# Row sums moved to ScalarE's accumulator, and two transposes moved ahead of the output projection, in an attention and FFN layer

## The reference

```
def layer(x):
    n = (x - mean(x)) / sqrt(var(x) + 1e-5)
    q, k, v = n @ Wq + bq, n @ Wk + bk, n @ Wv + bv      # 8 heads of 128
    # attention inside blocks of 64 tokens only
    scores = einsum('bnqhd,bnkhd->bhnqk', q, k) * 128 ** -0.5
    out = einsum('bhnqk,bnkhd->bnqhd', softmax(scores), v)
    x = x + out @ Wo + bo
    n = (x - mean(x)) / sqrt(var(x) + 1e-5)
    y = square(relu(n @ W_fc.T)) @ W_proj.T              # 4096 hidden
    mem, total = 0, 0
    for _ in range(5):
        reset = mem > 1
        mem = 0.9 * mem + y - reset
        total += mem > 1
    return x + total / 5
```

## Time and profile before

| | |
|---|---|
| Median of 2 runs | 1156.52 us (1153.59 to 1159.45) |
| Profiled execution, its own time | 1153.43 us |
| Span of its slowest core (core 2) | 1151.9 us |
| Spans of the 8 cores | 1132.4 to 1151.9 us |
| PE, DVE, ACT, POOL busy | 833.4, 485.1, 393.3, 254.0 us |
| Attention stage on core 2 | from 0 to about 540 us |

### The profile page before, as it was taken

The page is one execution under the profiler, slowest core; times in us unless marked ns, Lnnn a source line. Parts: engine busy times, 40 slices in busy tenths (PEclk is TensorE's granted clock), DMA queues, the critical chain, the costliest instruction groups (busy, mean ns, idle before and its releaser), DMA issues.

```text
span 1151.9 us, 19025 instructions; the slowest of 8 cores (1132.4 to 1151.9 us)
## 1 busy us (share of the span) xinstructions
PE 833.4 (72%) x6624; PEld 603.6 (52%) x6624; DVE 485.1 (42%) x513; ACT 393.3 (34%) x841; POOL 254.0 (22%) x122
## 2 busy tenths in 40 slices
PE   0098459943896379746997979879798897979910
PEld 0044324432343234432786868768687786868800
DVE  0303431153204430434005639275491855739186
ACT  1032323232232313121444444544444444454400
POOL 3000100010000100000003516153260633516154
PEclk9999559955997579859898999999899998999955
DMA  9994770057203640176686949789495996959600
GB/s 155 197 228 78 146 146 1 2 101 144 49 1 72 128 94 0 27 148 192 180 278 198 309 155 316 230 255 326 168 309 188 309 299 200 321 162 324 234 37 37
DMA packets 127291, 194.20 MB, mean 169 GB/s; under 512 B 42208, under 2 KB 44256, under 8 KB 127200
## 3 DMA queue, kind: packets, MB, share of 16 engines
q1 hardware_dynamic: 108144, 151.03, 43.3%
q0 software_dynamic: 14448, 33.56, 16.2%
q10 hardware_dynamic: 4608, 8.39, 2.0%
HBM read 192.95 MB, written 25.17 MB: 189 GB/s over the span
## 4 chain that ended last, share of the span: by engine, by line
PE 60%; DMA 18%; DVE 10%; ACT 5%; issue 4%; SPq 1%; POOL 1%; DVEq 0%; ACTq 0%; POOLq 0%
PE psC L802 17%; DMA w2scratch<-w2stage 10%; PE psA L836 9%; PE psB L836 8%; DMA w1slab<-w1scratch 5%; DMA bv_sb<-bv 3%; PE psA L604 3%; PE psA L336 3%; PE psB L604 2%; PE psB L375 2%; PE psA L356 2%; PE psB L336 2%; PE psA L375 2%; PE psB L356 2%; DVE mem_q L907 2%
## 5 line engine op out<-in xcount | busy, mean ns | idle before, releaser
L802 PE MATMUL psC<-xn2t_sb,w1slab 128*128 128x256 bf16 x2048 | 276.5, 281 | 16.8 <-ACT xn2t_sb L740 10.5
L802 PEld LDWEIGHTS psC<-xn2t_sb,w1slab 128*128 128x128 bf16 x2048 | 205.2, 101 | 48.7 <-issue 19.8
L813 ACT ACTIVATE h_bf<-psC 128x256 bf16<-128x256 f32 x256 | 97.6, 381 | 225.6 <-PE psC L802 225.4
L836 PE MATMUL psA<-h_bf,w2slab 128*128 128x256 bf16 x1024 | 156.1, 276 | 25.2 <-ACT h_bf L816 22.5
L903 POOL TENSOR_TENSOR acc_q<-acc_q,spk_q 128x2048 bf16<-128x2048 bf16 (+1 forms) x27 | 148.4, 5495 | 72.4 <-DVE spk_q L899 72.4
L836 PE MATMUL psB<-h_bf,w2slab 128*128 128x256 bf16 x1024 | 155.7, 275 | 0.0
L907 DVE SCALAR_TENSOR_TENSOR mem_q<-mem_q,y_sb 128x2048 f32<-128x2048 f32 (+1 forms) x27 | 142.9, 5291 | 2.8
L836 PEld LDWEIGHTS psA<-h_bf,w2slab 128*128 128x128 bf16 x1024 | 98.8, 98 | 45.2 <-issue 33.3
L816 ACT ACTIVATE h_bf<-h_bf 128x256 bf16<-128x256 bf16 x256 | 106.7, 417 | 24.1 <-ACT h_bf L813 0.7
L836 PEld LDWEIGHTS psB<-h_bf,w2slab 128*128 128x128 bf16 x1024 | 101.3, 99 | 12.8
L218 POOL DMA_DIRECT2D wtmp<-Wfc x32 | 17.0, 533 | 378.7 <-PE psD L499 350.0
(11 more groups left out here) (95 smaller groups left out, 1000.5 us busy)
## 6 DMA issues: line engine op xcount, KB each, us to landing
w2slab<-w2scratch SPq DMA_DIRECT2D x128, 512.0 KB, 6.8
w1slab<-w1scratch SPq DMA_DIRECT2D x128, 512.0 KB, 7.9
x_sb<-x SPq DMA_DIRECT2D x4, 2048.0 KB, 45.1
wtmp<-Wpr POOLq DMA_DIRECT2D x16, 512.0 KB, 6.4
wtmp<-Wfc POOLq DMA_DIRECT2D x32, 256.0 KB, 7.4
w2scratch<-w2stage SPq DMA_DIRECT2D x32, 256.0 KB, 4.1
w1scratch<-w2stage ACTq DMA_DIRECT2D x32, 256.0 KB, 5.4
out<-x_sb POOLq DMA_DIRECT2D x16, 512.0 KB, 8.1
```

Source lines behind the costliest of these rows:

```text
L802: op("pe", lambda E, fc=fc, c=c, hp=hp, s1b=s1b: E.matmul(hp, s1b[:, c * 128:(c + 1) * 128], xn2t_sb[:, c * 256:(c + 1) * 256], start=(c = ...
L813: op("se", lambda E, fc=fc, hp=hp: E.activation(h_bf[fc % 2][:], hp, ACT.Relu), inc="se")
L836: E.matmul(tgt[:, mc * 256:(mc + 1) * 256], slb[:, m * 128:(m + 1) * 128], h_bf[fp % 2][:], start=(fp == 0 and m % 2 == 0), stop=(fp == 31 ...
```

## The change

There are three edits.

1. In `ln1_part1` the row sum leaves DVE: ACT runs an Identity activation over the row with `accum_out` (it writes into `xn1_bf`, which the Square overwrites), and then the Square as before. DVE no longer waits for the load of `x`.
2. In `exp4_h` one Exp of 256 columns becomes four of 64, each with `accum_out`, so that ACT makes the four sums. The DVE reduction in `softmax_post` is gone.
3. Groups 0 and 1 of the next panel's transposes stand before the output projection (and before PE's wait for the last head), groups 2 and 3 behind its quarters 0 and 1.

```diff
@@ ln1_part1
         if jj == 0:
-            wait("ve", *E_xp[p])
             wait("se", *E_xp[p])
             wait("se", "pe", E_xn1t_fill_prev[0])
-        op("ve", lambda E, xtj=xtj: E.reduce_sum(
-            sums[:, jj:jj + 1], xtj, AX.X), inc="ve")
-        wait("ve", "ve", n["ve"])
+        op("se", lambda E, xtj=xtj, xoj=xoj: E.activation(
+            xoj, xtj, ACT.Identity, accum_out=sums[:, jj:jj + 1]),
+            inc="se")
+        wait("se", "se", n["se"])
@@ exp4_h
-            op("se", lambda E, h=h: E.activation(
-                s_f32[h % 3][:],
-                psC[:, (h % 2) * 512:(h % 2) * 512 + 256],
-                ACT.Exp), inc="se")
+            c0 = (h % 3) * 4
+            for g in range(4):
+                op("se", lambda E, h=h, g=g, c0=c0: E.activation(
+                    s_f32[h % 3][:, g * 64:(g + 1) * 64],
+                    psC[:, (h % 2) * 512 + g * 64:
+                        (h % 2) * 512 + (g + 1) * 64],
+                    ACT.Exp, accum_out=ssum[:, c0 + g:c0 + g + 1]),
+                    inc="se" if g == 3 else None)
@@ softmax_post
-            op("ve", lambda E, g3=g3, c0=c0: E.tensor_reduce(
-                ssum[:, c0:c0 + 4], g3, AX.X, ALU.add), inc="ve")
-            wait("ve", "ve", n["ve"])
@@ end of a panel
+        if p + 1 < PA:
+            xn1t_group(p + 1, 0)
+            xn1t_group(p + 1, 1)
         wait("pe", "ve", E_attnev[7])
         for jj in range(4):
...
-            if p + 1 < PA:
-                xn1t_group(p + 1, jj)
+            if p + 1 < PA and jj < 2:
+                xn1t_group(p + 1, jj + 2)
```

More of the change, by code:

```diff
@@ L425, in softmax_post @@
                 wait("ve", "pe", E_pt[h - 3])
-            g3 = s_f32[h % 3][:].rearrange("p (g k) -> p g k", g=4)
-            op("ve", lambda E, g3=g3, c0=c0: E.tensor_reduce(
-                ssum[:, c0:c0 + 4], g3, AX.X, ALU.add), inc="ve")
-            wait("ve", "ve", n["ve"])
             op("ve", lambda E, c0=c0: E.reciprocal(
@@ L432, in softmax_post @@
             wait("ve", "ve", n["ve"])
+            g3 = s_f32[h % 3][:].rearrange("p (g k) -> p g k", g=4)
             op("ve", lambda E, h=h, g3=g3, c0=c0: E.tensor_tensor(
```

## The result

The changed kernel takes 1143.3 us (median of 11 runs) against 1155.7 us for the kernel before (10 runs): ratio 0.9878, 95% interval 0.9858 to 0.9899. The ratio compares the means of the fast runs, 1142.1 and 1156.1 us (one of the 11 was slow, 1213.7 us), a gain of 14.1 us. The forecast was 1143 us, range 1137 to 1152, "within 2%". The sum was right, and so was the sign of each of its five terms, but two of its terms were mis-sized, and the loop's gain does not sit where the prediction put it.

What follows compares the result with a forecast made beforehand. The head loop was taken to be bound by a chain of DVE's copy L536 and the single staging buffer's write. 5.2 + 5.5 + 0.3 - 1.8 + 2.2 = 11.4 us off 1153.4, plus 1 us for run spread: 1143, range 1137 to 1152.

Steps and rivals of the forecast that it cites:

- five terms: Sum of gains: start 5.2 us, loop in panels 0 to 2 5.5, panel 3 0.3, Exps -1.8, moved transposes 2.2.
- The start: Panel 0's LN1: with row sums on ACT, L257 follows the last bias at once, at 46.65 us; 5.2 us gained.
- The cover named: At the start the late bias covers ACT's extra 4 us; an early bias would make them cost about 4 us.
- The short and the long intervals: Head loop, panels 0 to 2: short intervals gain 0.75 and 0.3 us, long ones 0.4 each; 5.5 us in all.
- ACT in the loop at nothing: Head loop: ACT's added LN activations and longer Exp cost nothing; without cover, up to 1.3 us at six places, 8 us.
- sign that everything would be wrong: Head loop: ACT's copies L510 or L453 becoming the releasers of PE would make everything wrong.
- Four Exps for one: Start of each head loop: a group ends after 1.1 us; about 0.45 us lost per panel, 1.8 us in four.
- The moved transposes: Panel's end: 1.36 us wait gone, 0.5 lost to a later start; 0.75 us taken per panel, 2.2 in three.
- The write stays the bound: Head loop, rival: earlier W_proj load takes the chain's gain from the even write; 5.6 us off, about 1149; chance 0.23.
- The loop gains all: Head loop, rival: even writes land in time, 11.4 us instead of 5.5, 17.3 off, 1137; chance 0.10.
- Transposes leave the clock down: Panel's end, rival: cold stretch begins only behind the transposes; 0.95 us worse in three panels, 1146; chance 0.16.
- Accumulator reads cost more: Head loop starts, rival: dearer Exp pieces make the kernel slower from 0.6 us more each; 1161 at x = 3; chance 0.05.

## Why the prediction was right

**The start.** Right: forecast 5.2 us, measured 5.4 from the rows and 4.7 by the run with this part alone. (The prediction put L257 at 46.65 us, 0.27 behind L208; it came 0.10 behind.) The cover named was the right one, and its price too: about 4 us without it was forecast, 4.8 came.

**The short and the long intervals.** The total was 1.85 us per panel by forecast, 2.5 in the profiles, and 4.5 to 6.3 us for three panels (1.5 to 2.1 each) by the runs that put edit 1 in or out of the loop. The distribution failed, and that the total came out is in part luck: two wrong sizes made up for each other. I gave the short intervals 0.75 and 0.3 us less and the long ones 0.4 each. In fact the short ones gained nothing (0.4 and 0.5 longer in the profile of the changed kernel, unchanged within 0.2 in the three others) and the long ones 1.6 and 2.0. The step that failed is the weight between the two effects that I had both named. For the collision of the even step's write with the load that now comes 1.9 us earlier I had allowed 0.14 us (5.0 instead of 4.86); the write takes 1.2 us longer, 5.4 instead of 4.3 at step 2. The median over all steps, in the page's list of DMA issues, rose from 4.1 to

```profile
w2scratch<-w2stage SPq DMA_DIRECT2D x32, 256.0 KB, 5.0
```

so that DVE waits for it in the short interval, in 40 of 48 cases against 12; and the odd step's write, which runs beside less of that load, takes 7.1 and 8.0 us instead of 8.8 and 10.0. What left DVE's path was paid out by the DMA engines, one interval later. The run without W_proj loads shows that it is the load that makes the long intervals long. That its earlier start is what shortens them fits the two measured shifts (1.9 us earlier, 1.8 us shorter), but was not tried by moving the load alone.

**ACT in the loop at nothing.** Half right. PE does wait for ACT's L454 behind L511 and the two LN activations, 27.4 us in all on core 2 ahead of `w2_group`; with the waits ahead of `w1_group` it is 33.5 us, where it was 9.2 before. The prediction had named this as a sign that everything would be wrong, and it was not: that sign was badly chosen. It had looked at the short interval, where the wait comes behind `w2_group`. The one that bites is in the even steps, where `w2_group` itself needs the half that `ptev` releases. It seldom sets the pace, though: in 41 of 48 cases DVE's copy waits for the slow write even longer, and part of PE's wait is not the activations but L511's own wait for the W_fc write (3.51 us in panel 0 above). The run with the sums back on DVE shows that the exchange is still worth 6.3 us.

**Four Exps for one.** The bounds held, 0.93 us for the group against 1.1 forecast and 1.76 as the upper bound. The term of the sum was mis-sized: 0.45 us per panel was forecast (its own steps, 0.15 and 0.7 less 0.5, make 0.35), and in panels 1 to 3 the stretch grew by about 0.15 us. The last piece ends 0.55 us later than the single Exp did, and the DVE reduction that is gone took 0.5 of it at both Exps. Of the table's -1.0 us, 0.6 are panel 0's, whose first matmuls run at 1.2 GHz for a varying time.

**The moved transposes.** Right in sum: 0.66 us gained per panel against 0.75. Both parts were larger than forecast. From the first of PE's projection matmuls or early transposes to Q it is 21.06 us instead of 22.62, 1.56 gained where the wait of 1.36 was named, and that first one starts 0.90 us later, not 0.5 (means of 24 panel ends). The question was whether the clock's cold stretch begins with the transposes. Over 24 panel ends, before: quarter 0 of the projection (from its first matmul to the transposes behind it) takes 6.34 us, 2.05 more than a warm one (4.29). After: the two groups take 1.77 us, 0.85 more than warm, and quarter 0 takes 5.50, 1.2 more: together 2.05. The same loss is spread over the transposes and fewer matmuls. The granted clock itself rose from 0.50 to 1.00 in the mean 4.4 us behind the first projection matmul before the change, and 4.3 us behind the first transpose after it (single panel ends lie between 2.3 and 5.9 us). The Trainium skill (TensorE: Matmul & The Clock Gate, Part 4: PE-mode transpose) says that transposes don't count for the clock as matmuls do. By that rule quarter 0 would have stayed at 6.34 us; it took 5.50, so the trace disagrees.

**The rivals.** "The write stays the bound" was half the truth (the short intervals) and yet no loss. "The loop gains all" fell short. "Transposes leave the clock down" would have lost 0.2 us per panel; 0.66 were gained. "Accumulator reads cost more" did not happen: 0.20 us for a piece.

**The number.** That 1143.3 us meets the forecast of 1143 to a third of a microsecond is luck. The forecast took 11.4 us off an assumed 1154.4; the medians are 12.5 us apart and the means 14.1, from a kernel before that took 1155.7.

## What to carry to other kernels

When work leaves an engine's path and a transfer is next on it, look at what that engine's progress releases: here the load that started earlier went with a slower write beside it and a faster next one, and the gain turned up an interval later than where the work was taken out. A gain that is hidden by a late arrival (here the bias) is a gain only as long as the arrival is late; name the cover and try it away. And judge a wait by putting the work back, not by its length in the profile: 27 us of PE waiting for ACT stood beside a gain of 6 us, and doubling a buffer whose writes DVE waits 75 us for (the page's group of L537 after the change) was worth nothing alone.

## What the runs showed of the hardware

Reading ACT's accumulator was cheap where activations followed each other: four Exps of 64 columns with their reads end 0.93 us after the start, where one of 256 takes 0.38 us. The read was counted at 0.19 us in the profile, but a pair of activation and read took only 0.20 from start to start.

Transposes on PE counted for TensorE's clock as the matmuls behind them did: 2.05 us lost in both orders, mean of 24 panel ends, and the clock rose 4.3 us behind the first transpose as it had 4.4 us behind the first matmul.

A 256 KB write from SBUF to HBM landed 8.8 to 10.0 us after the copy when a 512 KB load of W_proj was issued beside it (steps 3 and 5), and 3.1 to 4.0 us after it when these loads were left out.

Of the three tiny bias vectors (4 KB each, issued behind a 2 MB load of x) the last landed at 41 to 48 us after the start, where the load of x landed at 11 to 14; it held back the first PE work by 31 us (54.7 against 23.7 with the wait moved).
